# Loading the first quarter of an adjacency matrix in single tiles instead of pairs, with the waits and fillers of the matmul engine rewritten to match

## The reference

```
x = layernorm(x + L0(x, adj))   # weights from a running count over each row of adj, last 100 neighbours
x = layernorm(x + L1(x, adj))   # two gated graph convolutions: m = adj @ (x @ W), then a GRU cell
x = layernorm(x + L2(x, adj))   # normalised adjacency product, then W
x = layernorm(x + L3(x, adj))   # mean over neighbours, concatenated, then W
```

```
rank = cumsum(adj != 0, axis=1);  deg = rank[:, -1:];  k = min(deg, 100)
pos  = rank - (deg - k)
w    = mask * where(pos > 0, 0.5 ** (k - pos), 0)
out  = w @ (x @ weight) + bias
```

## Time and profile before

| | busy us | share of the span | instructions |
|---|---|---|---|
| TensorE matmul | 408.3 | 95% | 2307 |
| TensorE weight load (beside the matmuls) | 195.8 | 46% | 2322 |
| VectorE | 300.0 | 70% | 860 |
| ScalarE | 206.7 | 48% | 329 |
| GpSimd | 114.8 | 27% | 154 |

### The profile page before, as it was taken

One profiled execution on the slowest core, in us unless ns is written; L12 is line 12 of the kernel. 1 busy time (PEld: TensorE's weight loads), 2 busy tenths in 40 slices (PEclk: granted clock), 3 DMA queues, 4 the chain that ended last, 5 costly groups with the idle time before them and its releaser, 6 DMA issues.

```text
span 430.3 us, 6494 instructions
## 1 busy us (share of the span) xinstructions
PE 408.3 (95%) x2307; PEld 195.8 (46%) x2322; DVE 300.0 (70%) x860; ACT 206.7 (48%) x329; POOL 114.8 (27%) x154
## 2 busy tenths in 40 slices
PE   6977989999999999999999999999999999999991
PEld 2332433434344444445555555555544444444480
DVE  3387968966976787475966557876948666477773
ACT  2566788688868867407745335434223121212100
POOL 8213223222310100024221313334325434311111
PEclk9999999999999999999999999999999999999997
DMA  8999999999999993362110200000000101200000
GB/s 145 107 115 107 107 108 107 107 108 107 109 107 108 107 108 37 83 64 42 24 26 12 39 0 2 0 2 0 2 0 14 24 14 24 27 12 26 24 24 14
DMA packets 24959, 23.61 MB, mean 55 GB/s; under 512 B 14520, under 2 KB 16344, under 8 KB 24928
## 3 DMA queue, kind: packets, MB, share of 16 engines
q0 software_dynamic: 9360, 16.78, 39.0%
q1 hardware_dynamic: 15424, 6.36, 7.5%
q10 hardware_dynamic: 144, 0.07, 0.1%
HBM read 69.32 MB, written 1.06 MB: 164 GB/s over the span
## 4 chain that ended last, share of the span: by engine, by line
PE 79%; DMA 7%; DVE 5%; POOL 4%; issue 3%; ACT 1%; POOLq 0%; DVEq 0%
PE Y L1067 45%; PE both L976 14%; DMA adjT<-in_adjT 7%; PE both L955 3%; PE Y L955 3%; PE both L983 2%; PE both L924 2%; PE both L927 2%; PE both L967 2%; PE Y L967 2%; POOL rstd L282 1%; POOL adjT L310 1%; PE both L918 1%; PE both L931 1%; ACT wgt L392 1%
## 5 line engine op out<-in xcount | busy, mean ns | idle before, releaser
L1067 PE MATMUL Y<-adjT,S 128*128 128x512 fp8e4 (+1 forms) x1056 | 231.2, 373 | 0.9 <-DVE S L562 0.8
L1067 PEld LDWEIGHTS Y<-adjT,S 128*128 128x128 f16 x1056 | 101.6, 98 | 109.3 <-POOL S L297 1.2
L392 ACT ACTIVATE wgt<-both,consts 128x512 int16<-128x512 f32 x160 | 106.8, 687 | 33.5 <-PE both L976 29.4
L282 POOL TENSOR_TENSOR rstd<-stat,mhalf 128x4 f32<-128x4 f32 (+2 forms) x29 | 35.1, 1211 | 152.3 <-DVE stat L502 152.3
L976 PE MATMUL both<-adjT,tri 128*128 128x512 fp8e4 x160 | 60.6, 380 | 2.9 <-DMA adjT<-in_adjT 2.7
L976 PE MATMUL both<-adjT,fix 128*128 128x512 fp8e4 x152 | 58.0, 381 | 2.0 <-ACT wgt L392 1.5
L310 POOL DMA_DIRECT2D adjT<-in_adjT x63 | 35.8, 587 | 80.7 <-DMA adjT<-in_adjT 80.5
L522 DVE SCALAR_TENSOR_TENSOR work<-Y,yT 64x512 f32<-64x512 f32 x30 | 20.8, 695 | 46.6 <-ACT yT L353 46.2
L353 ACT ACTIVATE yT<-Y 64x512 f32<-64x512 f32 x30 | 17.6, 587 | 71.0 <-PE Y L1067 46.3
L976 PEld LDWEIGHTS both<-adjT,fix 128*128 128x128 bf16 x152 | 14.7, 97 | 37.2 <-ACT wgt L392 22.7
L364 ACT ACTIVATE work<-work 64x512 f16<-64x512 f32 x30 | 18.8, 627 | 26.6 <-DVE work L522 25.2
(11 more groups left out here) (124 smaller groups left out, 458.7 us busy)
## 6 DMA issues: line engine op xcount, KB each, us to landing
adjT<-in_adjT POOLq DMA_DIRECT2D x63, 256.0 KB, 39.0
out_rows<-xrow SPq DMA_DIRECT2D x7, 128.0 KB, 1.9
xrow<-in_xrow SPq DMA_DIRECT2D x1, 640.0 KB, 7.3
x<-in_w_gates SPq DMA_DIRECT2D x1, 512.0 KB, 5.5
biases<-in_biases SPq DMA_DIRECT2D x1, 384.0 KB, 4.4
x<-S SPq DMA_TRANSPOSE x24, 2.5
xrow<-in_xrow SPq DMA_DIRECT2D x1, 256.0 KB, 3.7
adjT<-in_adjT POOLq DMA_DIRECT2D x2, 128.0 KB, 7.7
```

The source lines that it names most:

```text
L282: nc.gpsimd.tensor_tensor(rstd[:, 0:blocks], stat[:, 2, 0:blocks], mhalf[:, 0:blocks], ALU.pow)\
L392: nc.scalar.activation(wgt[:, c, tiles % 2, :], V[c][:, :], ACT.Relu, bias=tile_bias[sums]).then_inc(w_ready[c], 1)
L1067: mm = nc.tensor.matmul(bank(layer, g)[:, 0:nb * P], S[layer % 2][:, jb, :], cols[:, jb, :], start=(jb == 0), stop=(jb == JB - 1), skip_gr ...
```

## The change

Four things are changed.

1. In quarter 0 every pair is loaded in two DMAs of one tile each, tile 2jp+1 first. It signals `first_tile[i]`, one semaphore for each of the 16 pairs; tile 2jp signals `load[i]`.
2. Pairs 8 to 23 wait for pair i-8 in addition: so 16 single-tile DMAs are under way in quarter 0, and 8 pairs at the start of quarter 1. From pair 24 on it is 16 pairs again.
3. The waits follow. In quarter 0 TensorE waits for `first_tile[i]` ahead of an odd tile and for `load[i]` ahead of an even one; `sum_quad` waits for four semaphores instead of two.
4. `BETWEEN` is rewritten. In quarter 0 the constant matmuls are 8, 18 and 8 (at steps 1, 4 and 14) instead of 8, 13 and 3 (at 1, 4 and 10), and one masked product moves half a step ahead. In quarters 2 and 3 the same products of layer 1 stand at slightly other places, with one more of them inside quarter 2 and one fewer after quarter 3.

```diff
-        first_tile = sem("first_tile")
+        first_tile = [sem(f"first_tile{i}") for i in range(JP)]
...
                     if i >= NLOAD:
                         pool.wait_ge(load[i % NLOAD], 16 * (i // NLOAD))
+                    if JP // 2 <= i < JP + JP // 2:
+                        pool.wait_ge(load[(i - JP // 2) % NLOAD], 16)
                     jp = ORDER[q][n]
-                    if i == 0:
-                        for half, landed in ((1, first_tile), (0, load[0])):
+                    if q == 0:
+                        for half, landed in ((1, first_tile[i]), (0, load[i])):
...
                     dve.wait_ge(load[i % NLOAD], 16 * (i // NLOAD + 1))
-                    if i == 0:
-                        dve.wait_ge(first_tile, 16)
+                    if q == 0:
+                        dve.wait_ge(first_tile[i], 16)
...
-                {(1, 0): ((8,),), (4, 0): ((13,),), ... (8, 0): ((6, 2, 0), (6, 2, 1)), ... (10, 0): ((3,),), (15, 1): ...
+                {(1, 0): ((8,),), (4, 0): ((18,),), ... (7, 1): ((6, 2, 0), (6, 2, 1)), ... (14, 0): ((8,),), (15, 1): ...
...
-                            if i == 0 and at % 2 == 1:
-                                pe.wait_ge(first_tile, 16)
-                            elif i == 0 or at % 2 == 1:
+                            if q == 0 and at % 2 == 1:
+                                pe.wait_ge(first_tile[i], 16)
+                            elif q == 0 or at % 2 == 1:
                                 pe.wait_ge(load[i % NLOAD], 16 * (i // NLOAD + 1))
```

## The result

The changed kernel took 434.53 us (median of five executions, 434.33 to 434.78) against 432.54 (five executions, 432.48 to 433.26): ratio 1.0041, 95% interval 1.003 to 1.0053. It is slower by 2.0 us. That lies inside the range of 431.9 to 435.0, but the likeliest case, no measurable change, was missed, and so was its own range (432.2 to 433.6). That the time fell inside the wider range is luck: its upper part stood there for rivals A and D, and neither of them happened.

A forecast was written before the change was run, and what follows sets the result against it. Quarter 0's loads up to pair 11 were taken to set when dense matmuls begin. Stream 0.3, TensorE's wait 0.09 and VectorE's 0.05 gave 0.44 us, so 432.9; range 431.9 to 435.0, own range 432.2 to 433.6.

The forecast's parts named there:

- Rival A: Quarter 0's load stream: 1 KB packets do not hide their overhead, 0.33 us per pair, 437.3; 12% at full or half price.
- Rival D: Quarter 0, step 14: the eight constant matmuls end too late and push the count by up to 1.1 us, 434.0; 7%.
- What bounds it: Quarter 0 ends by pair 11's landing, VectorE's 1.6 us sum and 15.7 us of matmuls; from 96 us matmuls bound everything.
- Rival B: TensorE's head start on pair 9 reaches quarter 0's end, capped at 0.35 us by pair 18: 432.2; 5%.
- The stream: Quarter 0's loads: smaller transfers cost 0.03 us more per pair, so pair 11 lands 0.3 us later (ends 0 and 3.6).
- C: The load stream gets faster by avoiding a disturbance; pairs 11 and 18 come up to 1.0 us sooner, 431.8; 8%.
- The waits: TensorE's added load wait at the even tile at 42.74 us costs 0.09 us (ends 0 and 0.36).
- VectorE's second wait: VectorE's sum of quad 2 in quarter 0 waits for `first_tile11` besides `load11`: 0.05 us (ends 0 and 0.09).
- the second pin: Start of quarter 1: pair 18 lands 0.35 us ahead of TensorE's first matmul; 0.45 us later, it adds nothing.
- the third: Quarter 1, 78.12 us: VectorE's sum of quad 2 starts just as pair 27 lands, 0.16 us idle ahead of it.
- Fillers, products: Quarter 0's added constant matmuls are hidden, some 0.4 us left at step 14; products moved in quarters 2 and 3 cost 0.
- GpSimd's issues: Fifteen more issues of 0.53 us each on GpSimd, covered by 16 single tiles in flight (19.7 us): cost nothing.

The follow-up runs named there:

- e6: The changed kernel with the old table of fillers and products (`BETWEEN`): 434.53 us, ratio 1.0036 to the kernel before.
- e7: The kernel before with the new table of fillers and products, loads and waits as before: 434.63 us, ratio 1.0038.
- e9: The changed kernel without the wait that holds 16 single tiles under way, so quarter 0's transfers are issued at once: 434.52 us, ratio 1.0046 to the kernel before.
- e1: The kernel before with 15 unused semaphores and 16 already satisfied waits on GpSimd added: 432.70 us, one execution.
- e8: The kernel before with neighbouring pairs joined into one transfer only where the consumer has slack, 47 transfers instead of 65: 431.35 us, ratio 0.9962.
- e4: The kernel before with 15 unused GpSimd loads of 16 rows, 16 bytes each, added behind its last load of `adjT`: 433.99 us, one execution.
- e5: The kernel before with neighbouring pairs joined into one transfer where wanted at once or early enough, 46 transfers instead of 65: 431.95 us, ratio 0.9982.
- e3: The kernel before with 15 unused GpSimd loads of 128 rows, 16 bytes each, added behind its last load of `adjT`: 434.25 us, ratio 1.0038.

## Why the prediction was right and wrong

**What bounds it: right, up to the last store.** Quad 2's sum, not TensorE's start on pair 9, set quarter 0's end. The start moved by 0.94 us and the count moved the other way. Rival B fell, and every later stretch up to 420 us kept its length within 0.3 us: the delay is 0.34 at the start of quarter 1, 0.60 from its sum of quad 4 on, 0.8 in quarter 3, 0.60 again from 185 us and 0.73 from 412 us.

**The stream: right in kind, small in size.** The term was 0.03 us per pair and measured 0.05 (2.51 against 2.46); its ends were 0 and 0.33. Packets of 1 KB do hide most of their overhead: 0.05 of the 0.33 us shows. For pair 11 the term was 0.3 us and the sum of quad 2 came 0.25 later; the prediction had 38.9, it was 38.83, so the agreement is partly luck: the price per pair was larger, and the disturbances on the way fell otherwise. Rival A (0.33 per pair, 437.3) fell, and so did C, a faster stream: neither landing 11 nor landing 18 came sooner. Landing 8 did (GpSimd's row at 31.48, of which 0.53 is reaction, against 31.88), and it was lost again by landing 11. The trace goes against the 2.0 us of fixed cost for each transfer that the Trainium skill's page "DMA: Bandwidth & Descriptors" gives under "Anatomy of one DMA", if these are simply added (an estimate of 30 us): 15 more transfers cost about 0.7 us in the stream and 1.23 at the end. Its direction, that more and smaller transfers cost time, was right, and the forecast gave it too little.

**The waits: 0.09 as predicted.** From the count to the extra wait, 40.11 to 42.74 before, the delay grows from 0.26 to 0.35: the even tile's matmul stands at 43.09 now. VectorE's second wait had 0.05; landing and sum both came 0.25 later, which leaves nothing for it: 0.

**A pin missed.** I had the second pin at pair 18 and the third at pair 27. Between them, pair 23 at the sum of quad 4 (68.29, 1.84 us idle ahead of it) is one too, and there TensorE's delay of 0.34 turned into the loads' 0.60. The 0.26 us are a mis-sized term, in that slack was looked for at two places only. Two things are in them: the loads were 0.44 late at landing 18 against TensorE's 0.34, and 0.16 more arose between landings 18 and 27, where both kernels load whole pairs. That 0.16 is within the scatter of the stream and is not shown to be the change's. Pair 18 landed 0.44 us later (55.99 to 56.43), as predicted (0.45).

**Fillers, products: right, with less to spare than I said.** e6 shows 0 for them. The count still follows VectorE's sum by 1.54 us, as it did before by 1.53, so the eight did not hold it. But the matmul behind them stands at 40.10, 0.27 us ahead of the count, where a dense step is 0.22: 0.05 us were left, not 0.4. Rival D needed a lost head start; e7 took it away and paid 1.7 us in the median, with the prediction's 1.1 at the edge of its interval. Its one trace adds 1.9 us of lower clock, for which the prediction had no term.

**The step that failed** is the cost of "GpSimd's issues. Fifteen more, 0.53 us each ... Costs nothing". While they run it is true: 16 tiles in flight cover them, and e9 shows that their moment does not matter. But each transfer has a second price, 0.082 us in GpSimd's DRAIN at the program's end, 1.23 us for fifteen. With it, the prediction's own sum would be 0.44 + 1.23 = 1.67 us, or 434.2 instead of 432.9; the 0.3 left is pair 23's 0.26 and the 0.13 near the end, less 0.05 each that pair 11 and VectorE's second wait cost below their terms. The prediction's last test, that a stretch changes by more than 0.3 us, was the one to catch it, although I had only the stretches up to 420 in mind.

**Open.** What GpSimd does in its DRAIN. The experiments vary the transfers together with the instructions that issue them, so they don't tell which of the two is paid for; e1 shows only that 16 satisfied waits and 15 semaphores are not. Whether a transfer issued by another engine would cost the same was not run. Nor was the number brought under 46. An estimate from the rows: SyncE has closed 2.9 us after the DRAIN starts (426.9 against 424.0 before), and a DRAIN is that short with some 25 transfers; fewer should gain nothing in this kernel. Nor was it tried to let GpSimd finish earlier, so that its DRAIN runs beside other work. Why 0.13 us more are lost between 406 and 412 us wasn't traced.

## What to carry to other kernels

Look at the closing DRAIN of each engine: which one ends last, and when does it start? Where it is GpSimd's, as here, count the transfers that GpSimd issues and price each at 0.08 us, whatever its size and however early it runs; splitting a load must give more than that on the chain, and joining loads pays where the consumer has slack (e8). Ask what a head start has to wait for next before counting it, and look for every place where the loads are the last to arrive, not for the nearest two. Fillers of TensorE that stand ahead of a wait take time where the wait has none left to cover them; before moving them, read the granted clock behind that wait in more than one profile, since here it fell behind idle times of 1.8 and 2.1 us in two profiles and not behind such ones in others.

## What was not expected of the hardware

- GpSimd's closing DRAIN grows with the number of transfers that GpSimd issued, by 0.082 us each, over 46 to 80 transfers and twelve profiles, from 4.58 to 7.35 us. Transfers of 256 bytes (e4) cost as much there as single tiles of 128 KB; 15 spare semaphores cost nothing (e1).
- The length of TensorE's idle time ahead of quad 3 does not alone decide whether its clock falls there. Behind 2.09 us (before) and 1.97 us (e4) it stayed at its upper level; in e5, with 2.10 us, it was 0.76 in 33 to 40 us, in e3, with 1.80 us, also 0.76, and in e7, with 2.73 us, 0.57. In e7 it fell while TensorE stood idle, in e5 and e3 after it had resumed (0.59 in 34.0 to 34.5 us, 0.84 in 35.5 to 36.0).
- A joined load of twice the size is not twice the issue on GpSimd: 0.72 us against 0.53 (e5, behind landings 19 and 27):

```profile
58.35 0.53 POOL L327 DMA_DIRECT2D adjT<-in_adjT  x1 [1.85 <-DMA adjT<-in_adjT]
...
78.35 0.72 POOL L329 DMA_DIRECT2D adjT<-in_adjT  x1 [4.18 <-DMA adjT<-in_adjT]
```
